# Layer 3 of a four-layer graph network interleaved with the final loop of layer 2, on one core

## Reference

```
# layer 2
y = (adj @ h + h) @ weight + bias
y = y / max(norm(y, axis=2), 1e-12)
mean, var = masked mean and variance of y over all graphs and nodes, per feature
x = x + relu(((y - mean) / sqrt(var + 1e-5) * gamma + beta) * mask)
# layer 3
h = relu(layernorm(x))
x = x + tanh(concat(h, adj @ h) @ W1 + b1) @ W2 + b2
```

## Time and profile before

| | us |
|---|---|
| median of 3 runs | 1465.61 |
| lowest and highest | 1465.5, 1466.25 |
| the profiled execution's own time | 1463.7 |
| its span, first to last instruction | 1462.0 |
| mean granted TensorE clock | 0.966 |

### The profile page before, as it was taken

The page is one execution under the profiler, slowest core; times in us unless marked ns, Lnnn a source line. Parts: engine busy times, 40 slices in busy tenths (PEclk is TensorE's granted clock), DMA queues, the critical chain, the costliest instruction groups (busy, mean ns, idle before and its releaser), DMA issues. The chain is left out here.

```text
span 1462.0 us, 41154 instructions
## 1 busy us (share of the span) xinstructions
PE 1316.5 (90%) x11243; PEld 1076.8 (74%) x11244; DVE 1154.9 (79%) x2874; ACT 1105.1 (76%) x2426; POOL 502.5 (34%) x611
## 2 busy tenths in 40 slices
PE   3999999999999999999999999997999997972398
PEld 1777777877777777777777777875889887910298
DVE  7898988899888988889888998883444445978755
ACT  4788888888888888888888888863555555916676
POOL 1343344444443344444433444431222111066400
PEclk9999999999999999999999999997999998986599
DMA  7000000000000000000000000000000000000022
GB/s 154 22 10 9 8 7 14 7 7 7 7 14 7 7 7 14 7 7 7 7 14 7 7 7 7 0 2 1 0 0 0 0 0 0 0 1 0 4 54 57
DMA packets 40925, 18.11 MB, mean 12 GB/s; under 512 B 19572, under 2 KB 40886, under 8 KB 40886
## 3 DMA queue, kind: packets, MB, share of 16 engines
q1 hardware_dynamic: 40354, 17.42, 4.8%
q10 hardware_dynamic: 532, 0.21, 0.1%
HBM read 13.44 MB, written 4.19 MB: 12 GB/s over the span
## 5 line engine op out<-in xcount | busy, mean ns | idle before, releaser
L723 DVE SCALAR_TENSOR_TENSOR acc<-slot_banks,acc 128x768 f32<-128x768 f32 x512 | 487.7, 953 | 79.5 <-PE slot_banks L442 70.6
L792 POOL TENSOR_TENSOR acc<-acc 128x384 f32<-128x384 f32 x128 | 128.1, 1001 | 529.1 <-DVE onediff L717 420.3
L442 PE MATMUL slot_banks<-ac_hi,work 128*128 128x192 f16 x1408 | 265.3, 247 | 27.3 <-DVE work L705 26.1
L442 PE MATMUL slot_banks<-ac_lo,work 128*128 128x192 f16 x1408 | 264.1, 246 | 0.0
L442 PEld LDWEIGHTS slot_banks<-ac_hi,work 128*128 (+1 forms) x1408 | 137.4, 98 | 98.4 <-issue 76.1
L442 PE MATMUL slot_banks<-ac_hi,onediff 128*128 128x192 f16 x1024 | 183.1, 246 | 6.4 <-DVE acc L723 5.1
L442 PE MATMUL slot_banks<-ac_lo,onediff 128*128 128x192 f16 x1024 | 182.3, 246 | 0.0
L442 PEld LDWEIGHTS slot_banks<-ac_lo,work 128*128 (+1 forms) x1408 | 138.2, 98 | 20.2 <-issue 14.5
L778 POOL TENSOR_TENSOR ac_lo<-ac,ac_hi 128x384 f16<-128x384 f32 x128 | 123.1, 961 | 49.3 <-ACT ac_hi L582 49.3
L542 ACT ACTIVATE work<-bank 128x512 f16<-128x512 f32 x256 | 130.7, 601 | 1.2 <-PE bank L353 1.2
L705 DVE TENSOR_SCALAR work<-work,slot_key 128x1024 f16 x256 | 117.9, 480 | 12.2 <-issue 3.7
(11 more groups left out here) (261 smaller groups left out, 3291.4 us busy)
## 6 DMA issues: line engine op xcount, KB each, us to landing
adj_in<-in_adj_dram SPq DMA_DIRECT2D x32, 256.0 KB, 2.8
out_dram<-acc SPq DMA_DIRECT2D x32, 128.0 KB, 2.0
l1w<-in_L_gnn_W_dram SPq DMA_DIRECT2D x2, 64.0 KB
l1b<-in_L_gnn_b_dram SPq DMA_DIRECT2D x2, 64.0 KB
x_all<-in_x_dram SPq DMA_DIRECT2D x4, 0.2 KB, 11.8
nm_in<-in_nodemask_dram ACTq DMA_DIRECT2D x1, 64.0 KB
w1a<-in_L_gnn_W_dram ACTq DMA_DIRECT2D x1, 48.0 KB
w1b<-in_L_gnn_W_dram ACTq DMA_DIRECT2D x1, 48.0 KB
```

What stands on the lines that cost most here:

```text
L442: last = nc.tensor.matmul(unit(pair, t, 1), hot(t), part[:, q, H:2 * H].unsqueeze(1), start=False, stop=(e == 1 and (t % SB == SB - 1 or t ...
L723: nc.vector.scalar_tensor_tensor(out=sums, in0=unit((q + k) % 2, 0, SU), scalar=0.0, in1=sums, op0=ALU.min, op1=ALU.add).then_inc(s_free[k ...
L792: nc.gpsimd.tensor_tensor(acc[:, q, 0:2 * H], acc[:, q, 0:2 * H], acc[:, q, 2 * H:4 * H], ALU.add)
```

## The change

Layer 3's block is merged into the block with layer 2's batch norm. Its PE loop is as before. DVE, ACT and POOL now follow written-out orders, `fold_in`, `fold_in_act` and `shifts_and_roots`, in which iteration i of layer 3 (two groups, so the eight graphs of chunk i) stands beside work of layer 2 on later chunks: the add to `x` of chunk i + 5, the ReLU of chunk i + 6, the scaling of chunk i + 8. Five chunks are finished before layer 3 starts. All adds to `x` are DVE's now; POOL keeps the shift by beta.

Layer 3's scales are made for three chunks (24 graphs) at a time, in six batches. DVE makes the variances, POOL raises them to the power -1/2, and DVE does one Newton step on that estimate, then the offset. So ACT needs no square root there, and the table for tanh is loaded once, ahead of the ReLUs.

The scales for layers 1 and 2 are made in two parts: graphs 0 to 95 (`most`) during the layer before, graphs 96 to 127 (`last_ones`) at the start of the layer, while ACT already normalises the first two groups.

```
@@ layer 0, ScalarE and VectorE steps @@
+        most, last_ones = slice(0, 3 * B // 4), slice(3 * B // 4, B)
...
+                    if known(b) and b == B - GS + 1:
+                        layernorm_std(act, 3, most)
...
+                        if known(b) and b == B - GS:
+                            layernorm_var(dve, 3, most)
+                        if known(b) and b == B - GS + 1:
+                            layernorm_rstd(dve, 3, most)
@@ layer 1 @@
-                layernorm_std(act, 3)
                 act.wait_ge(s_ln, 3)
                 for u in range(2):
                     for q in range(GS):
                         norm_h1(u, GS * u, q)
+                layernorm_std(act, 4, last_ones)
+                act.wait_ge(s_ln, 4)
 
...
                 with act.Fori(0, NI - 1) as i:
                     group_pair(i, True)
+                layernorm_std(act, 5, most)
                 group_pair(NI - 1, False)
...
-                layernorm_scales(dve, 3)
+                layernorm_var(dve, 4, last_ones)
+                layernorm_rstd(dve, 4, last_ones)
...
-                with dve.Fori(1, NI) as i:
+                with dve.Fori(1, NI - 1) as i:
                     group_pair(i, i - 1)
+                dve.wait_ge(s_bn1, 3 * NI // 4)
+                layernorm_var(dve, 5, most)
+                layernorm_rstd(dve, 5, most)
+                group_pair(NI - 1, NI - 2)
@@ layer 2 @@
-                layernorm_std(act, 4)
-                act.wait_ge(s_ln, 4)
+                act.wait_ge(s_ln, 5)
                 for u in range(2):
                     for q in range(GS):
                         norm_graph(s_hn2[u], u, GS * u, q, q == GS - 1)
+                layernorm_std(act, 6, last_ones)
+                act.wait_ge(s_ln, 6)
...
-                layernorm_scales(dve, 4)
+                layernorm_var(dve, 6, last_ones)
+                layernorm_rstd(dve, 6, last_ones)
@@ batch norm and layer 3 @@
-        AHEAD = 3
...
+        LEAD = 6
+        QC = 3
+        NB = (NXC + QC - 1) // QC
+        minus_half = sb("minus_half", [N, QC * GX])
...
+        def scale_chunk(c):
+            nc.vector.tensor_tensor(g3(yc(c)), g3(yc(c)), per_feature(stat[:, 5, :]), ALU.mult).then_inc(s_ya, 1)
+        def shift_chunk(pool, c):
+            pool.wait_ge(s_ya, c + 1)
+            nc.gpsimd.tensor_tensor(g3(yc(c)), g3(yc(c)), per_feature(beta[:, :]), ALU.add).then_inc(s_yb, 1)
+        def add_to_x(dve, c):
+            v = nc.vector
+            dve.wait_ge(s_yc, 2 * c + 2)
+            v.tensor_tensor(xc(c), xc(c), yc(c), ALU.add).then_inc(s_xn, 1)
+            dve.wait_ge(s_xn, c + 1)
+            for e in range(GX):
+                last = stats(c * GX + e)
+            last.then_inc(s_bn2, 1)
+        def batch(k):
+            return slice(k * QC * GX, min((k + 1) * QC, NXC) * GX)
+        def variances(dve, k):
+            v = nc.vector
+            cols = batch(k)
+            m0, q0, m1, q1 = (bn6[:, cols, t] for t in (1, 2, 4, 5))
+            dve.wait_ge(s_bn2, min(QC * k + QC, NXC))
+            v.tensor_tensor(msum[:, cols], m0, m1, ALU.add)
+            v.tensor_tensor(var[:, cols], q0, q1, ALU.add)
+            v.tensor_tensor(dif[:, cols], m0, m1, ALU.subtract).then_inc(s_lnq, 1)
+            dve.wait_ge(s_lnq, 6 * k + 1)
+            v.tensor_scalar(var[:, cols], var[:, cols], 1.0 / F, EPS, ALU.mult, ALU.add)
+            v.scalar_tensor_tensor(out=dif[:, cols], in0=dif[:, cols], scalar=0.25, in1=dif[:, cols],
+                                   op0=ALU.mult, op1=ALU.mult).then_inc(s_lnq, 1)
+            dve.wait_ge(s_lnq, 6 * k + 2)
+            v.tensor_tensor(var[:, cols], var[:, cols], dif[:, cols], ALU.add).then_inc(s_lnq, 1)
+        def scales(dve, k):
+            v = nc.vector
+            cols = batch(k)
+            root, error = std[:, cols], dif[:, cols]
+            dve.wait_ge(s_root, k + 1)
+            v.scalar_tensor_tensor(out=error, in0=root, scalar=-0.5, in1=root, op0=ALU.mult, op1=ALU.mult)             .then_inc(s_lnq, 1)
+            dve.wait_ge(s_lnq, 6 * k + 4)
+            v.tensor_tensor(error, error, var[:, cols], ALU.mult).then_inc(s_lnq, 1)
+            dve.wait_ge(s_lnq, 6 * k + 5)
+            v.scalar_tensor_tensor(out=rstd[:, cols], in0=error, scalar=1.5, in1=root, op0=ALU.add, op1=ALU.mult)             .then_inc(s_lnq, 1)
+            dve.wait_ge(s_lnq, 6 * k + 6)
+            v.scalar_tensor_tensor(out=nmr[:, cols], in0=msum[:, cols], scalar=-0.5, in1=rstd[:, cols],
+                                   op0=ALU.mult, op1=ALU.mult).then_inc(s_ln3, 1)
+        def shifts_and_roots(pool):
+            g = nc.gpsimd
+            def shifts(first, past):
+                for c in range(first, past):
+                    shift_chunk(pool, c)
+            def inverse_root(k):
+                cols = batch(k)
+                pool.wait_ge(s_lnq, 6 * k + 3)
+                g.tensor_tensor(std[:, cols], var[:, cols], minus_half[:, 0:cols.stop - cols.start], ALU.pow)\
+                 .then_inc(s_root, 1)
+            g.memset(minus_half[:, :], -0.5).then_inc(s_minus, 1)
+            pool.wait_ge(s_minus, 1)
+            shifts(0, LEAD - 1)
+            inverse_root(0)
+            shifts(LEAD - 1, LEAD + 2)
+            for k in range(1, NB):
+                inverse_root(k)
+                shifts(min(QC * k + LEAD - 1, NXC), min(QC * k + QC + LEAD - 1, NXC))
+        def fold_in(dve):
+            v = nc.vector
+            def copy_sums(i, u):
+                dve.wait_ge(s_agg3[u], i + 1)
+                v.tensor_copy(msg[:, u, :], bank[4 * u][:, :]).then_inc(s_aggs3[u], 1)
+            def update(i, u):
+                if i > 0:
+                    dve.wait_ge(s_out[u], 16 * i)
+                v.tensor_tensor(upd[:, u, :].rearrange("p (q f) -> p q f", q=GS),
+                                x[:, ds(GS * grp(u, i) * F, GS * F)].rearrange("p (q f) -> p q f", q=GS),
+                                l3b2[:, :].unsqueeze(1).broadcast_to([N, GS, F]), ALU.add).then_inc(s_xb[u], 1)
+                dve.wait_ge(s_dh[u], i + 1)
+                dve.wait_ge(s_xb[u], i + 1)
+                v.tensor_tensor(upd[:, u, :], bank[4 * u + 2][:, 0:GS * F], upd[:, u, :], ALU.add)\
+                 .then_inc(s_new[u], 1)
+            for c in range(3):
+                scale_chunk(c)
+            for c in range(LEAD - 1):
+                add_to_x(dve, c)
+                if c == QC - 1:
+                    variances(dve, 0)
+                if c + 3 <= LEAD + 1:
+                    scale_chunk(c + 3)
+            scales(dve, 0)
+            copy_sums(0, 0)
+            for i in range(NI):
+                copy_sums(i, 1)
+                if i > 0:
+                    update(i - 1, 1)
+                if i + LEAD - 1 < NXC:
+                    add_to_x(dve, i + LEAD - 1)
+                if (i + 2) % QC == 0 and (i + 2) // QC < NB:
+                    scales(dve, (i + 2) // QC)
+                last = i + LEAD - 1
+                if last == NXC - 1 or (last < NXC and last % QC == QC - 1):
+                    variances(dve, last // QC)
+                if i + 1 < NI:
+                    copy_sums(i + 1, 0)
+                update(i, 0)
+                if i + LEAD + 2 < NXC:
+                    scale_chunk(i + LEAD + 2)
+            update(NI - 1, 1)
+        def fold_in_act(act):
+            def masked_relu(c, half):
+                act.wait_ge(s_yb, c + 1)
+                for b in range(c * GX + half * GX // 2, c * GX + (half + 1) * GX // 2):
+                    yb = y[:, b * F:(b + 1) * F]
+                    last = act.activation(yb, yb, ACT.Relu, scale=nm[:, b:b + 1])
+                last.then_inc(s_yc, 1)
+            def norm_group(i, u):
+                if u == 0 and i % QC == 0:
+                    act.wait_ge(s_ln3, i // QC + 1)
+                for q in range(GS):
+                    norm_graph(s_hn3[u], u, GS * grp(u, i), q, q == GS - 1)
+            nc.scalar.activation(cnt_col[:, 0:1], eps_col[:, 0:1], ACT.Tanh)
+            for c in range(LEAD - 1):
+                masked_relu(c, 0)
+                masked_relu(c, 1)
+            norm_group(0, 0)
+            norm_group(0, 1)
+            masked_relu(LEAD - 1, 0)
+            masked_relu(LEAD - 1, 1)
+            for i in range(NI):
+                for u in range(2):
+                    if i + 1 < NI:
+                        act.wait_ge(s_agg3[u], i + 1)
+                        norm_group(i + 1, u)
+                    act.wait_ge(s_lin3[u], i + 1)
+                    nc.scalar.activation(hid[:, u, 0:2 * N], bank[4 * u + 1][:, 0:2 * N], ACT.Tanh,
+                                         bias=l3b1[:, 0:1]).then_inc(s_tanh[u], 1)
+                    if i + LEAD < NXC:
+                        masked_relu(i + LEAD, u)
 
...
-                def scale(c):
-                    v.tensor_tensor(g3(yc(c)), g3(yc(c)), per_feature(stat[:, 5, :]), ALU.mult).then_inc(s_ya, 1)
```

(39 more changed lines are left out.)

170 lines of the change are left out of this document (63 added, 107 removed).

## The result

| | before | after |
|---|---|---|
| median | 1465.55 us (4 runs, 1463.8 to 1466.25) | 1446.26 us (4 runs, 1445.43 to 1448.59) |
| profiled execution | 1463.7, span 1462.0 | 1445.43, span 1443.7 |

The ratio is 0.9881, with a 95% interval of 0.9863 to 0.9899: 19.3 us faster, where the prediction said 7.1.

The account below looks back on a forecast made before the run. DVE was taken to bound layer 2's final loop and the merged loop, PE layer 3's old loop. Terms -5.4 (merge), -3.2, -0.3 (layer starts) and +1.8 (layer 0) sum to -7.1, giving 1458.5 us, range 1451.5 to 1465.5.

Parts of the forecast that it names:

- the merge: Layer 3 beside layer 2's final loop: -24.4 us before the loop and +19.0 in it, together -5.4.
- the five adds: Adds to x before layer 3's loop, each counted at 1.67 us beside a POOL shift; uncertainty -5 to +5 us.
- layer 0's +1.8: Layer 0's last iterations: DVE's extra variances, reciprocals and offsets cost between 0 and 2.7 us, taken as +1.8.
- they share: Overlapping DVE and POOL instructions are both lengthened, 0.65 to 1.67 us and 1.26 to 1.71.
- this rival: One engine blocks the other: adds before and in the loop wait out a shift, +2.3 us, so 1460.8; chance 0.03.
- Less contention: Rival: the shift runs beside statistics and copies only, -5 us before the loop, -2 in it, 1452; chance 0.12.
- The total of 5.97 for an iteration: DVE's work in a full merged-loop iteration: 5.47 us of parts plus about 0.5 for the shift, used for iterations 0 to 7.
- the loop turns on ACT: Rival: ACT, not DVE, sets the merged loop's pace, some 7.1 us for ten iterations, +6.5, so 1465; chance 0.17.
- PE at half clock in the loop: Rival: gaps cost PE its clock grant in the merged loop, +34 us, or +17 and 1475 for half; chance 0.10.
- The power: POOL's power for layer 3's scales, taken as 1 us, free up to 5.5; rival that it is long, chance 0.08.
- Layer starts: Layers 1 and 2 begin normalising at once because scales of 96 graphs are ready: -3.2 and -3.3 us.
- Layer 1's last pair: Layer 1's last iteration: the early square root waits for DVE's variances, +2.7 us, plus 0.3 for a lower clock.

Follow-up runs that it names:

- the scaled chunk in the middle: The changed kernel with DVE's scaled chunk put between the add to x and its statistics; median 1445.58 us, ratio 0.9883.
- the halved ReLUs: The changed kernel with layer 2's mask and ReLU left out for half of each chunk's graphs; one execution, 1447.78 us.

## Why the prediction was wrong in size

Its sign, its structure and what sets the pace held. The time did not: 1446.26 is 12.2 below 1458.5. In the profiled executions the merge gave 7.8 more, the rest 3.4 more (together 11.2). No single step carries this. Before the loop it is 2.4: 5.1 too much for the five adds, against 3.1 that the scales cost beyond their price. In the loop it is 5.4, of parts priced a little high, of shifts that delay nothing in four iterations of eight, and of its last iterations. Outside the merge it is mostly layer 0's +1.8, which did not come, and the clocks. The five adds are the largest term by itself, and there the mechanism was wrong.

**The step that failed: "they share".** The prediction took 0.65 for an undisturbed DVE instruction and 1.67 beside a shift, and counted the five adds before the loop at 1.67 because "the chunk scaled just ahead of it has started a shift". The runs show exclusion, and in it the order decides. An instruction that is delayed ends 0.55 after the other engine's (512 columns), 0.28 (256 columns) or 0.04 (24 columns). Each is 0.12 to 0.14 less than its row's length alone (0.68, 0.41, 0.18), so about its own length without what the row reaches into the next:
-: the shift from 1338.49 ends at 1340.20, the scaled chunk from 1340.02 at 1340.75: 0.55.
- after: three shifts end at 1327.76, the first add at 1328.31: 0.55. The shift from 1362.20 ends at 1363.47, L1557 at 1363.75: 0.28.

So the evidence stood in the earlier trace rows. The two lengths there, 1.67 and 1.71, come from alternation: POOL had adds of its own, and each engine always found the other inside. POOL's 1.71 is its own 1.26 plus 0.45 of waiting. Rows that are both longer looked like sharing; the ends of the rows, not their lengths, tell the two apart. The prediction gave this rival 0.03 and turned it down because POOL's rows were stretched; but POOL is stretched too whenever DVE was first. Its price, +2.3, was wrong as well, since it made the add the loser every time. In the new order the second and third add begin 0.16 before the shift (1329.97 and 1330.13), the fourth and fifth stand beside the power, and only the first loses. So the shift waits, and nobody waits for the shift. Of the rivals it was *Less contention* (0.12) that had the sizes, -5 for the adds and -2 in the loop, where -5.1 and -1.2 were measured; its reason, that the shift runs beside statistics and copies only, holds because the shift was made to wait, and its 1452 is still 5.7 too high.

The Trainium skill, page SBUF — State Buffer, section Who interferes with whom, has this as its rule: the first to issue holds the port for its whole instruction and the other is blocked. The trace agrees (0.95 and an unchanged 1.26; 0.68 and 1.64), and the prediction's sentence that it does not was wrong: it took the longer POOL rows for sharing, when POOL had been the one that waited. By that section a DVE instruction with at most one SBUF input, outside the two-port modes, is left out of this: the PSUM copy at 1362.04, with the shift from 1362.20 beside it, took 0.68, so this agrees as well. Other rows go against its word that a DVE instruction with two SBUF inputs contends with a GpSimd instruction that reads SBUF, and that the first holds the port throughout: beside the power (1373.04 to 1377.21) L1557 took 0.42 and the add 0.68, as if alone. So did the others in after: 18 instructions of these two lengths lie wholly inside a power, and none took more than 0.72. Why the power differs from the shift stayed open.

**Before the loop** the prediction had 24.3 from the first scaled chunk to the first normalisation, measured are 21.85:
- Five adds with statistics and scaled chunks: 12.5 instead of 17.65, -5.1.
- Variances 0.86 instead of 1.2, -0.3; the first add 4.49 after the first scaled chunk instead of 4.56, -0.1 (it waits 1.54 for ACT here, while in the earlier trace rows DVE's own four scaled chunks reach to it; that the two times agree is luck).
- The scales, from 1340.35 to 1344.31: 3.96 instead of 0.9, +3.1. This is the same exclusion at the place where it hurts. Three shifts are queued behind the power, and DVE's three small products each wait for one. The prediction had named 24 columns as cheap and looked only at their own length.

The way from there to iteration 0's copy was 6.16, as predicted (6.1).

**In the loop** 85.8 instead of 91.2. Rebuilt from the rows, a plain iteration without contention is 5.25, where the prediction's 5.47 had each part a little high (0.60 for the scaled chunk, 0.71 instead of 0.84 for the add with its wait). The shift costs 0.70 where it meets L1557, not 0.5, giving 5.95, but it does so only in iterations 2, 3, 5, 6 and 8. In iterations 1, 4 and 7 POOL is at the power, and in iteration 0 no shift runs. Variances cost 0.99 and scales 0.93. So 5.25 + 0.70 + 0.99 = 6.94 and 5.25 + 0.93 = 6.18, which are the measured lengths. Over iterations 0 to 7:
- 8 x 0.22 of parts, -1.8;
- contention 4 x 0.70 instead of 8 x 0.5, -1.2;
- small instructions, -0.5.

That is 49.7 instead of 53.2. Iteration 8 is DVE's as well (5.36, a contended 5.96 without the 0.60 of the scaled chunk), not ACT's. Iterations 8 to 10 and 11 to 14 took 1.5 and 0.4 less. The total of 5.97 for an iteration was nearly exact, 5.95, with two errors in it that cancelled where both stood (parts 0.22 too high, contention 0.20 too low); it was the eightfold use of it that did not hold.

**ACT** needs 5.28 per iteration, not 5.74, as the 5.28 from tanh to tanh show in the iterations that DVE does not hold (with the scaled chunk in the middle, iterations 2, 5 and 8). The rival that the loop turns on ACT is refuted by the halved ReLUs. **PE at half clock in the loop** did not come about: 1.00 throughout.

**The power** was taken at 1 us and is 4.17. Nobody waited for it, because the prediction had worked out how much would be hidden: "up to that length it costs nothing", 5.5 us. That was luck in part, since 4.17 is above the upper row that I had called nearest, 1.71. And its length has effects that the prediction did not look for. In iterations 1, 4 and 7 it keeps the shift away from L1557, 0.70 each. Before the loop it holds back the shifts of chunks 5, 6 and 7 until all three stand beside the scales; how much of the 3.1 there a short power would have spared, no run tells.

**Layer starts**: 3.43 earlier at layer 1 and 3.43 at layer 2 from the block to PE's first product, predicted 3.2 and 3.3. **Layer 1's last pair**: +2.7 and 0.3 for the clock were predicted, it is 20.50 instead of 16.44, +4.06, with the named cause (ACT's wait of 2.98, PE's gap of 2.30) and a clock of 0.85 after it. So the gap was 2.30 where 2.7 was taken, and the other 1.8 is what comes after it at the lower clock, where 0.3 was taken from a range of 0 to 3. The kernel that makes the square root later gets 4.05 of it back. **Layer 0** was charged 1.8 for DVE's extra work and paid nothing that can be seen: its last accumulation starts at 995.48, inside the 994.72 to 996.19 of all kernels. The prediction named the reason for zero itself (DVE's gaps there answer PE) and then did not take it.

**The signs** that the prediction named as making it wrong (a power over 5 us, a clock below 1 in the loop, ACT at 100%) did not appear, and it was wrong all the same. Three of those that it named as showing it did not come: the adds at 1.7 were 0.68, the first normalisation at about 1350 was at 1344.31, and the copies every 6.0 to 7.2 were 5.4 to 6.95 apart.

**Left over** are -2.85 in layer 1, -1.45 at the end of layer 0 and +2.09 in the batch norm. In all three the granted clock goes with it, as the tables by stretches show. What puts an execution into the one or the other clock stayed open.
